# An attention stage of a graph kernel: all clamps on GpSimd as a minimum and a maximum, one count product per key tile, four whole tiles in the ring

## The reference

```python
q = (embeds[rows] @ qW).reshape(e, HEADS, dh)          # 4 heads of 24
k = (embeds[cols] @ kW).reshape(e, HEADS, dh)
v = (embeds[cols] @ vW).reshape(e, HEADS, dh)
scores = jnp.clip(jnp.einsum('ehd,ehd->eh', q, k), -10.0, 10.0)
exp_s = jnp.exp(scores)
norms = jax.ops.segment_sum(exp_s, rows, num_segments=nvar)[rows]
w = exp_s / (norms + 1e-08)
res = jax.ops.segment_sum(w[:, :, None] * v, rows, num_segments=nvar).reshape(nvar, d)
return embeds + res
```

## Time and profile before

| what | value |
|---|---|
| time, median of 3 runs (lowest, highest) | 1285.33 us (1283.32, 1286.96) |
| the profiled execution's own time | 1289.9 us |
| its span, first to last instruction | 1287.9 us |
| mean granted TensorE clock | 0.904 |
| PE / PEld busy | 1053.3 / 622.0 us |
| DVE / ACT / POOL busy | 966.7 / 692.6 / 597.2 us |
| attention, first exponential to start of the last values | 424.4 to 877.5 us |
| POOL floors L985 | 175, 430.8 us |
| DVE products L1151 and floors L1145 | 350, 366.8 us, and 88, 63.0 us |
| ACT exponentials L1120, relus L1116, exponentials L1118 | 263, 87 and 87; 251.7, 95.0 and 90.7 us |
| PE scores L1065, values L1075, counts L1054 | 184.9, 170.8 and 68.7 us |

### The profile page before, as it was taken

How to read it: one execution, slowest core, us unless ns; L and a number is a source line. 1 busy time by engine, 2 the same in 40 slices (tenths; PEclk the granted TensorE clock), 3 DMA queues, 4 the chain that set the end, 5 groups by cost and what they waited for, 6 DMA issues and landing times.

```text
span 1287.9 us, 23338 instructions
## 1 busy us (share of the span) xinstructions
PE 1053.3 (82%) x8352; PEld 622.0 (48%) x8352; DVE 966.7 (75%) x1603; ACT 692.6 (54%) x903; POOL 597.2 (46%) x343
## 2 busy tenths in 40 slices
PE   3878877778886788888888888994799699999893
PEld 2545545445553222222222222231569699999783
DVE  8668888896664799999999999994865654542566
ACT  7556555555533899999979898992100000001221
POOL 8442454233103799999989998995000000000000
PEclk9878888977687799999989999997899899999896
DMA  0010000000016211121111222221000100010201
GB/s 10 26 40 5 5 8 6 5 5 18 2 42 189 68 38 46 45 49 47 42 44 36 60 52 51 46 59 48 1 1 32 37 29 21 2 33 8 68 28 38
DMA packets 98907, 44.80 MB, mean 35 GB/s; under 512 B 85196, under 2 KB 96716, under 8 KB 98672
## 3 DMA queue, kind: packets, MB, share of 16 engines
q1 hardware_dynamic: 97104, 41.58, 12.2%
q0 software_dynamic: 1696, 1.74, 0.5%
HBM read 30.73 MB, written 12.56 MB: 34 GB/s over the span
## 4 chain that ended last, share of the span: by engine, by line
PE 52%; DVE 25%; issue 12%; ACT 5%; POOL 4%; another core or an unknown queue 2%; DMA 1%; SPq 0%; DVEq 0%; ACTq 0%; POOLq 0%
DVE Eb L1151 16%; PE PS L1325 16%; PE PS L553 11%; PE PS L557 8%; DVE Eb L1145 3%; PE PS L1765 3%; POOL Eb L985 3%; PE PS L1333 2%; PE PS L1075 2%; PE PS L1065 2%; ACT Eb L1116 2%; PE PS L1316 1%; ACT Eb L1118 1%; PE PS L1772 1%
## 5 line engine op out<-in xcount | busy, mean ns | idle before, releaser
L985 POOL TENSOR_SCALAR Eb<-Eb 128x1024 f32<-128x1024 f32 (+4 forms) x175 | 430.8, 2483 | 42.0 <-ACT Eb L1120 40.8
L1151 DVE SCALAR_TENSOR_TENSOR Eb<-Eb,PS 128x1024 f32<-128x1024 f32 (+4 forms) x350 | 366.8, 1084 | 16.4 <-ACT Eb L1118 10.1
L1120 ACT ACTIVATE Eb<-PS,small 128x1024 f32<-128x1024 f32 (+2 forms) x263 | 251.7, 997 | 27.2 <-PE PS L1065 23.4
L593 ACT ACTIVATE CT<-PS 128x500 f32 x313 | 183.5, 587 | 147.1 <-PE PS L557 139.3
L553 PE MATMUL PS<-mov,oneS 128*128 128x100 f16 x1565 | 187.8, 235 | 74.1 <-issue 70.5
L553 PEld LDWEIGHTS PS<-mov,oneS 128*128 128x128 f16 x1565 | 148.4, 109 | 159.1 <-issue 118.0
L1325 PE MATMUL PS<-hs,CT 128*128 128x192 f16 (+1 forms) x2500 | 213.5, 247 | 3.6 <-DVE SG L1566 1.6
L1325 PEld LDWEIGHTS PS<-hs,CT 128*128 128x128 f16 (+1 forms) x2500 | 208.1, 99 | 7.3 <-DVE SG L1566 2.4
L1065 PE MATMUL PS<-Qb,Kb 96*128 96x512 f16 (+3 forms) x700 | 184.9, 368 | 10.5 <-ACT Eb L1120 6.8
L435 DVE TENSOR_TENSOR oneS<-iotaX,KL 128x2560 f16<-128x2560 int16 x80 | 120.0, 1500 | 75.1 <-PE PS L557 73.0
L1075 PE MATMUL PS<-Eb,V 128*25 128x512 f32 (+3 forms) x1400 | 170.8, 560 | 3.4 <-DVE Eb L1151 1.8
(11 more groups left out here) (278 smaller groups left out, 1017.3 us busy)
## 6 DMA issues: line engine op xcount, KB each, us to landing
Kb<-kd SPq DMA_DIRECT2D x168, 96.0 KB, 2.3
qd<-QH SPq DMA_DIRECT2D x12, 192.0 KB
kd<-QH SPq DMA_DIRECT2D x12, 192.0 KB
hs<-t_d SPq DMA_DIRECT2D x12, 192.0 KB, 2.5
Qb<-qd SPq DMA_DIRECT2D x4, 384.0 KB, 3.8
CT<-x_d SPq DMA_DIRECT2D x1, 1200.0 KB, 9.1
x_d<-B SPq DMA_DIRECT2D x6, 192.0 KB, 1.9
t_d<-A SPq DMA_DIRECT2D x6, 192.0 KB, 1.8
```

What stands on the lines that cost most here:

```text
L593: a.activation(K.CT[:, :, bass.ds(words[g % 4][0], GI * W)], K.bank(g % 4)[:, 0:25 * GI * W].rearrange("p (a c) -> p a c", a=25), ACT.Copy ...
L985: g.tensor_scalar(e, e, ELO, None, ALU.max).then_inc(S("floored"), 1)
L1120: a.activation(e, ps, ACT.Exp, scale=K.unsc[0:r, :]).then_inc(S("score_read"), 1)
L1151: v.scalar_tensor_tensor(out=e, in0=e, scalar=EHI, in1=cn, op0=ALU.min, op1=ALU.mult).then_inc(S("weighed"), 1)
```

## The change

`FLOOR`, the relu path on ACT and the floor on DVE go. ACT does one exponential for each half. POOL clamps every half in one instruction of two operations, minimum with exp(10) and maximum with exp(-10). DVE multiplies a whole tile, four heads, by the counts in one `tensor_tensor`. `Eb` has four whole tiles in place of three, 32 KB a partition in place of 24, and ACT waits for the values of four tiles before. PE makes scores two tiles ahead in place of one; counts and values keep their place. The scratch for the indirect DMAs' descriptors is set to 8192.

```diff
-NE_ = 6
+NE_ = 4
-FLOOR = [("P", "A") if it % 2 else ("P", "D") for it in range(7 * NT)]
-    K.Eb = sb(st, "Eb", [128, NE_, 2, 512], F32)
+    K.Eb = sb(st, "Eb", [128, NE_, 4, 512], F32)
...
 def attn_gpsimd(g, K):
         for k in range(2):
-            if FLOOR[it][k] == "P":
-                e = K.Eb[0:r, (2 * it + k) % NE_, :, 0:wb]
-                g.wait_ge(S("score_read"), 2 * it + k + 1)
-                g.tensor_scalar(e, e, ELO, None, ALU.max).then_inc(S("floored"), 1)
+            e = K.Eb[0:r, it % NE_, 2 * k:2 * k + 2, 0:wb]
+            g.wait_ge(S("score_exp"), 2 * it + k + 1)
+            g.tensor_scalar(e, e, EHI, ELO, ALU.min, ALU.max).then_inc(S("clamped"), 1)
...
 def attn_tensor(p, K):
+    for it in range(2):
+        score(it, 0)
+        score(it, 1)
     count(0)
-    score(0, 0)
-    score(0, 1)
     for it, (b, t) in enumerate(ITS):
+        if it + 2 < len(ITS):
+            score(it + 2, 0)
+            score(it + 2, 1)
         if it + 1 < len(ITS):
-            score(it + 1, 0)
-            score(it + 1, 1)
             count(it + 1)
         if it:
             value(it - 1)
...
 def attn_scalar(a, K):
-            if it >= 3:
-                a.wait_ge(S("valued"), it - 3 + 1)
-            if FLOOR[it][k] == "A":
-                a.activation(e, ps, ACT.Relu, bias=K.ten[0:r, 0:1], scale=K.unsc[0:r, :]).then_inc(S("score_read"), 1)
-                a.wait_ge(S("score_read"), 2 * it + k + 1)
-                a.activation(e, e, ACT.Exp, bias=K.ten[0:r, 1:2]).then_inc(S("exp_a"), 1)
-            else:
-                a.activation(e, ps, ACT.Exp, scale=K.unsc[0:r, :]).then_inc(S("score_read"), 1)
+            if it >= NE_:
+                a.wait_ge(S("valued"), it - NE_ + 1)
+            a.activation(e, ps, ACT.Exp, scale=K.unsc[0:r, :]).then_inc(S("score_exp"), 1)
...
     def weigh(it):
-        cn = bcast_out(K.cntv[it % 2][0:r, 0:wb], 2, wb)
+        cn = bcast_out(K.cntv[it % 2][0:r, 0:wb], 4, wb)
         v.wait_ge(S("count"), it + 1)
-        for k in ((1, 0) if FLOOR[it][0] == "P" else (0, 1)):
-            e = K.Eb[0:r, (2 * it + k) % NE_, :, 0:wb]
-            kind = FLOOR[it][k]
-            if kind == "D":
-                v.wait_ge(S("score_read"), 2 * it + k + 1)
-                v.tensor_scalar(e, e, ELO, None, ALU.max).then_inc(step, own.up())
-                v.wait_ge(step, own.n)
-            elif kind == "P":
-                v.wait_ge(S("floored"), halves("P", it))
-            else:
-                v.wait_ge(S("exp_a"), halves("A", it))
-            v.scalar_tensor_tensor(out=e, in0=e, scalar=EHI, in1=cn, op0=ALU.min, op1=ALU.mult).then_inc(S("weighed"), 1)
+        e = K.Eb[0:r, it % NE_, :, 0:wb]
+        v.wait_ge(S("clamped"), 2 * it + 2)
+        v.tensor_tensor(e, e, cn, ALU.mult).then_inc(S("weighed"), 1)
...
-    nc = _bacc.Bacc("TRN2", target_bir_lowering=False, num_devices=1)
+    nc = _bacc.Bacc("TRN2", target_bir_lowering=False, num_devices=1, dynamic_dma_scratch_size=8192)
```

More of the change, by code:

```diff
@@ L927, in proj_tensor @@
     t.wait_ge(S("v_made"), 7)
-NE_ = 6
+NE_ = 4
 NK = 3
-FLOOR = [("P", "A") if it % 2 else ("P", "D") for it in range(7 * NT)]
-def halves(kind, it):
-    return sum(f.count(kind) for f in FLOOR[:it + 1])
 B0, BN = (0, 4, 8, 12, 16, 19, 22), (4, 4, 4, 4, 3, 3, 3)
@@ L948, in alloc_attn @@
     sb = K.sb
-    K.Eb = sb(st, "Eb", [128, NE_, 2, 512], F32)
+    K.Eb = sb(st, "Eb", [128, NE_, 4, 512], F32)
     K.accS = sb(st, "accS", [128, 512], F32)
     K.xb = sb(st, "xb", [128, 1, 4, D], F32)
-    K.ten = K.small[:, 100:102]
     K.rec = K.small[:, 104:136].rearrange("p (k c) -> p k c", k=2)
@@ L981, in attn_gpsimd @@
         for k in range(2):
-            if FLOOR[it][k] == "P":
-                e = K.Eb[0:r, (2 * it + k) % NE_, :, 0:wb]
-                g.wait_ge(S("score_read"), 2 * it + k + 1)
-                g.tensor_scalar(e, e, ELO, None, ALU.max).then_inc(S("floored"), 1)
-    g.wait_ge(S("floored"), halves("P", len(ITS)))
+            e = K.Eb[0:r, it % NE_, 2 * k:2 * k + 2, 0:wb]
+            g.wait_ge(S("score_exp"), 2 * it + k + 1)
+            g.tensor_scalar(e, e, EHI, ELO, ALU.min, ALU.max).then_inc(S("clamped"), 1)
+    g.wait_ge(S("clamped"), 2 * len(ITS))
 def gammas(g, K, i):
@@ L1050, in count @@
         if it >= 2:
-            p.wait_ge(S("weighed"), 2 * (it - 2) + 2)
+            p.wait_ge(S("weighed"), it - 1)
         for i in range(na):
@@ L1060, in score @@
         if it:
-            p.wait_ge(S("score_read"), 2 * (it - 1) + k + 1)
+            p.wait_ge(S("score_exp"), 2 * (it - 1) + k + 1)
         p.wait_ge(S("k_in%d" % (it % NK)), 16 * (it // NK + 1))
@@ L1070, in value @@
         b, t, wb, na, r = dims(it)
-        p.wait_ge(S("weighed"), 2 * it + 2)
+        p.wait_ge(S("weighed"), it + 1)
         if t == 0:
@@ L1074, in value @@
         for h in range(4):
-            m = p.matmul(bank(4)[32 * h:32 * h + 25, 0:wb], K.V[0:r, t, h, :], K.Eb[0:r, (2 * it + h // 2) % NE_, h % 2, 0:wb],
+            m = p.matmul(bank(4)[32 * h:32 * h + 25, 0:wb], K.V[0:r, t, h, :], K.Eb[0:r, it % NE_, h, 0:wb],
                          start=(t == 0), stop=(t == NT - 1), tile_position=(0, 32 * h))
@@ L1109, in attn_scalar @@
         for k in range(2):
-            e = K.Eb[0:r, (2 * it + k) % NE_, :, 0:wb]
+            e = K.Eb[0:r, it % NE_, 2 * k:2 * k + 2, 0:wb]
             ps = K.bank(2 * k, 2).rearrange("p (h c) -> p h c", h=2)[0:r, :, 0:wb]
             a.wait_ge(S("scores"), 2 * it + k + 1)
-            if it >= 3:
-                a.wait_ge(S("valued"), it - 3 + 1)
-            if FLOOR[it][k] == "A":
-                a.activation(e, ps, ACT.Relu, bias=K.ten[0:r, 0:1], scale=K.unsc[0:r, :]).then_inc(S("score_read"), 1)
-                a.wait_ge(S("score_read"), 2 * it + k + 1)
-                a.activation(e, e, ACT.Exp, bias=K.ten[0:r, 1:2]).then_inc(S("exp_a"), 1)
-            else:
-                a.activation(e, ps, ACT.Exp, scale=K.unsc[0:r, :]).then_inc(S("score_read"), 1)
-    a.wait_ge(S("score_read"), 2 * len(ITS))
-    a.wait_ge(S("exp_a"), halves("A", len(ITS)))
+            if it >= NE_:
+                a.wait_ge(S("valued"), it - NE_ + 1)
+            a.activation(e, ps, ACT.Exp, scale=K.unsc[0:r, :]).then_inc(S("score_exp"), 1)
+    a.wait_ge(S("score_exp"), 2 * len(ITS))
 def attn_vector(v, K):
@@ L1127, in attn_vector @@
     step = own.sem
-    v.memset(K.ten[:, 0:1], 10.0)
-    v.memset(K.ten[:, 1:2], -10.0).then_inc(step, own.up())
     v.memset(K.accS[:, :], 0.0).then_inc(step, own.up())
```

## The result

| what | before | after |
|---|---|---|
| median of the runs (lowest, highest) | 1286.14 us (1283.32, 1290.36), 4 runs | 1206.20 us (1204.06, 1210.93), 4 runs |
| span of the profiled execution | 1287.9 us | 1205.3 us |
| ratio, 95% interval | | 0.9375 (0.9353 to 0.9398) |

80 us are gone, where 68 were forecast (from the 1285.3 that was known then to 1217; 1206 came). The windows of the kernel after cut the span at the stage's borders; columns as in rows 3.

What follows compares the result with a forecast made beforehand. DVE and POOL were taken as the bound, ACT close behind. Fill 3.5 + products 361 + block ends 12 + clock 5 = 382 against 453, 71 less; from 1285.3 that gives 1214, plus 3 given back: 1217 us, range 1196 to 1290.

Steps and rivals of the forecast that it cites:

- The clamp: POOL, attention stage: a min-max pair on 128x1024 takes 1.04 to 1.15 us, 350 of them.
- the dear end: POOL's clamp of a half at 4.22 us, or 2.8 if the second operation is free.
- rival 1: POOL becomes the bound, clamps at the floor's price: 1695 us, or 2131 with a costed second operation; chance 0.14.
- DVE: DVE, attention stage: one product of 2048 at 2.29 us, 2.33 with the gap; 361 us over all tiles.
- PE and ACT: Loop of scores and exponentials in the attention stage: period 2.31 us a tile of 512, beside DVE's 2.33.
- Ring and scores past SP: Attention stage: four-tile ring has 1.5 us slack; scores passing SP's queue, which holds the K load, cost nothing.
- The scratch: Descriptor scratch of 8 KB for POOL's gathers: bounds 0 to 10 us, taken as 0.
- The sum: Attention stage: fill 3.5 + 361 + block ends 12 + clock 5 = 382 us against 453, 71 less.
- The 3 us given back for three engines at one level: Added to the forecast because POOL at 1.15 would need 2.30 a tile: 1214 becomes 1217.
- The three rivals: POOL as the bound, a middle clamp price, or PE taking the stall's place; chances 0.14, 0.05 and 0.03.
- a middle one: POOL's clamps at 1.64 ns an element, 580 us in all, 127 more: 1412 us; chance 0.05.
- not 2.7: PE takes the place of the stall at 2.7 us a tile, nothing gained: about 1283 us; chance 0.03.

Runs made afterwards that it cites:

- clamps alone: Kernel before with POOL clamping both halves as min-max pairs, one exponential and one product per half; ring of three, scores one tile ahead, old scratch: 0.9400.
- no_look: Changed kernel with scores one tile ahead instead of two; ring of four, whole products and pairs stay: 0.9706 of the kernel before.
- half_prod: Changed kernel with the count product as two instructions of a half each: 0.9371 of the kernel before.
- reorder: Changed kernel with PE's counts placed between the scores of the two halves: 0.9333 of the kernel before, 1192.3 us.
- after_again: Changed kernel run once more, unedited, on the same chip as three other runs: 0.9375 of the kernel before, 1198.6 us.
- the kernel before with pairs: Kernel before with only POOL's 175 floors turned into min-max pairs; the product still takes its minimum: 0.9944 of the kernel before.
- the run with one operation: Changed kernel with the minimum left out of POOL's clamp, leaving a lone maximum: 1670.7 us, one run.

## Why the prediction was right

By its own steps:

- *The clamp.* Right, and it carries all else. 1.04 to 1.15 us was taken for 1024 columns and 1.042 came; 0.83 ns an element was the memsets' slope and is the clamp's. The argument that led there, that one read could not cost more than two and the time must sit in the body, is borne out by 2.77 with VectorE idle. What it said of bodies was too simple: not the absence of a second operation makes it slow, as max-min and max-add cost 3.63. By its reason any second operation might have brought the quick body, and three of the five pairs tried don't have it. That the pair of this kernel, in this order, is one of the two quick ones was luck; nothing in the rows told it. The choice between 1.04 and 2.8 or 4.2 us was not forced by any row, and the dear end is real: for the pair in the other order a second operation adds 0.86 us to the 2.77. The dear end of the forecast had 1.42 for that, from an int32 row of 128 columns. The sentence that by the Trainium skill's second rule (GPSIMD Engine Reference, section 4.1) the time would be rival 1's does not follow: the same row of that page calls one-input work on GpSimd roughly line-rate, which is near the pair's 1.04 us and not the floor's 2.80.
- *DVE.* Right in the records: 2.29 us was worked out for 2048 elements, 2.277 came; 1.75 and 1.49 became 1.748 and 1.484. Wrong in the period: the 0.04 between instructions was not there. Four products after a block's end take 8.87 us, so with 2.277 for the last they start 2.20 apart and overlap by 0.08. Two products of 1.219 in 2.34 had shown the same before. DVE alone would have allowed 0.13 us a tile less than the forecast; it didn't matter, as PE's loop decides.
- *PE and ACT.* Right. The loop was worked out at 2.31 us a tile of 512, measured 2.285, with its parts: values 0.99, scores in pairs of 0.54 and 0.61. The run with the counts between the scores took that wait away, and the period fell to 2.20, close to the 2.17 of PE's work. (The scores are four times as many columns as the counts, four matmuls of 512 against four of 128; 2.6 is the ratio of their times. The 0.86 stands on 4 x 0.215 and not on that.)
- *Ring and scores past SP.* Right. With four tiles no exponential waits for values (ACT's 32.1 us of waits in the stage all end with a score), with three they do (1608 us). PE waits for a K load once, 7.2 us, at the stage's start; in the blocks it never does, as worked out.
- *The scratch.* Nothing, in its own run.
- *The sum.* 382 us were forecast for the stage and 372.7 came. The three periods make 100 x 2.285 + 50 x 1.83 + 25 x 1.655 = 361. The forecast's 361 was DVE's, 100 x 2.33 + 50 x 1.79 + 25 x 1.53; the measured one is PE's, 5 us less at 512 columns and as much more at the others. That the two sums agree is luck. The 9 us too many are the other terms: 3.5 for the fill, 12 for block ends and 5 for the clock came to 11 together. DVE's 2.20 lies 0.08 under PE's period, 2 us in the 25 tiles of a block, and so it can make good the time of a block end beside PE; this is worked out and was not tried. The granted clock of the stage was 0.99, so the 5 us for it were hardly spent. The 3 us given back for three engines at one level weren't needed either; and another 3 us fell away ahead of the stage. Against these 15 stand 1 us more behind the stage and the step from the profiled execution to the median: 4.6 was taken off for it, and it was 1.0 (1207.2 against 1206.2). That leaves 10 of the 11 between 1217 and 1206.

The three rivals are out: the clamp has 1.042 and neither the floor's price nor a middle one, and PE takes the bound at 2.285 and not 2.7. What the prediction did not see is how the gain divides. It priced the parts as one. The clamps alone bring the kernel to 0.940 of its time, the whole change to 0.9375. And the whole product, the ring and the scores ahead carry each other: take one away and 3% (scores) or 34% (ring) are lost, take product and scores back together and nothing is. The 3 us ahead of the stage are not the change's: on one chip the first exponential starts at 416.1, 416.3, 416.6 and 419.0 us in four runs that are the same up to there (`no_look`, `half_prod`, `reorder`, `after_again`).

```profile
741.05 0.85 PE L1065 MATMUL PS<-Eb,V 128*25 128x384 f32 x8
...
744.71 0.85 PE L1065 MATMUL PS<-Eb,V 128*25 128x384 f32 x8
...
780.70 0.74 PE L1065 MATMUL PS<-Eb,V 128*25 128x320 f32 x8
...
784.01 0.74 PE L1065 MATMUL PS<-Eb,V 128*25 128x320 f32 x8
```

These are starts two tiles apart, from which 1.83 and 1.655 come (timeline of the changed kernel).

## What to carry to other kernels

Measure the one instruction that a plan rests on by itself, in each form that computes the same: here the order of two constants decides between 1.04 and 3.63 us, and the price by the row of the same shape would have been wrong by a factor of 2.7. A quicker instruction on one of several full engines brings little (0.994 of the time); moving the others' work onto the room that it makes brings the gain (0.940). In an engine's list, put first what waits for nothing, and give the order one tile more of lookahead before moving a waiting instruction forward.

## What the runs showed of the hardware

- The addition of x1 on DVE, 384 columns with two inputs from SBUF, takes 0.558 us with no clamp beside it (at 576.28 in the kernel before with pairs), 0.979 in the changed kernel (mean of four, L1149 above), and 1.19 where it meets most of a clamp, as in the reordered kernel:

```profile
488.40 1.04 POOL L975 TENSOR_SCALAR Eb<-Eb 128x1024 f32<-128x1024 f32 x1
...
488.65 1.19 DVE L1150 TENSOR_TENSOR xb<-xb,accS 128x384 f32<-128x384 f32 x1
```

  It ends 0.40 us behind the clamp under way; with clamps alone the clamp ends 0.22 after the addition's start, and it takes 0.63. The Trainium skill (GPSIMD Engine Reference, section 1) names a DVE instruction with two SBUF inputs as one that contends with GpSimd; this agrees. A quick body as such does not make the difference: beside the slow floors it took 0.558 in the kernel before and 0.894 in the run with one operation, beside quick clamps 0.614 (clamps alone) to 1.187 (reordered), means of four. By these numbers the time goes with how much of a clamp it meets, and when; that was not tried by itself.
- PE's granted clock was 1.00 in the stretch from 500 to 575 us of the changed kernel, with PE busy 73.88 of 75 us, 0.94 in the first block before with 67.00 of 77 and 0.99 in the third with 63.54 of 75, and 0.68 in the run with three tiles, with 54.23. So the busy time of a stretch alone does not give the clock. In the run with three tiles the stalls cost their length and slower matmuls as well: it was forecast at 1470 and came at 1608.
